# Down projections by Strassen's scheme: seven half products in place of eight

## The reference

```python
scale = cond @ norm_w.T + 1.0
h = x * (scale[:, None, :] * rsqrt(mean(x * x) + EPS))
val, gate = split(h @ up_w.T, 2)              # FF = 2048
h = val * gelu(gate)
hq = act_quant(h)                             # per token, to 127 steps
wq = weight_quant(down_w)                     # -1, 0, +1 times a scale
y = hq @ wq.T + x                             # 2048 -> 512
# second block, per batch row: an adapter of width 128
Wd_b, Wu_b = Wd + dWd(cond), Wu + dWu(cond)   # dW = (cond @ Wdd.T + bdd) * 0.1
out = y + relu(y @ Wd_b.T + bd) @ Wu_b.T + bu
```

## Time and profile before

| | us |
|---|---|
| median of 3 runs | 850.45 |
| the profiled execution, span | 847.8 |
| TensorE busy | 834.7 |
| VectorE busy | 605.6 |
| ScalarE busy | 388.4 |
| GpSimd busy | 74.3 |
| down matmuls L1182, 384 of them, busy | 84.8 |

### The profile page before, as it was taken

The page is one execution under the profiler, slowest core; times in us unless marked ns, Lnnn a source line. Parts: engine busy times, 40 slices in busy tenths (PEclk is TensorE's granted clock), DMA queues, the critical chain, the costliest instruction groups (busy, mean ns, idle before and its releaser), DMA issues.

```text
span 847.8 us, 11801 instructions
## 1 busy us (share of the span) xinstructions
PE 834.7 (98%) x3982; PEld 366.9 (43%) x3982; DVE 605.6 (71%) x904; ACT 388.4 (46%) x633; POOL 74.3 (9%) x79
## 2 busy tenths in 40 slices
PE   6999999999999999999999999999999999999998
PEld 4334444444444444444444444444444444444443
DVE  5998787989877765658776656668975664445986
ACT  5778887775454532237454542126333332224000
POOL 0363332202000000002000000000200000000100
PEclk9999999999999999999999999999999999999999
DMA  9879988665999843377889754436246444432232
GB/s 342 333 269 339 348 285 300 235 224 209 323 350 373 305 149 117 116 255 274 294 308 335 270 200 134 151 106 211 84 133 217 137 162 141 140 117 77 99 123 76
DMA packets 64426, 183.49 MB, mean 216 GB/s; under 512 B 7024, under 2 KB 8304, under 8 KB 64368
## 3 DMA queue, kind: packets, MB, share of 16 engines
q1 hardware_dynamic: 64080, 182.48, 61.7%
q10 hardware_dynamic: 288, 0.26, 0.1%
HBM read 152.31 MB, written 29.36 MB: 214 GB/s over the span
## 4 chain that ended last, share of the span: by engine, by line
PE 93%; DVE 1%; issue 0%; DVEq 0%
PE aux_ps L1182 10%; PE b_ps L1082 9%; PE b_ps L1086 9%; PE b_ps L1084 9%; PE a_ps L1082 6%; PE a_ps L1086 6%; PE a_ps L1084 6%; PE aux_ps L1137 6%; PE aux_ps L1233 3%; PE aux_ps L1224 3%; PE c_ps L1086 3%; PE c_ps L1082 3%; PE c_ps L1084 3%; PE e_ps L1082 3%; PE e_ps L1086 3%; PE e_ps L1084 3%
## 5 line engine op out<-in xcount | busy, mean ns | idle before, releaser
L1590 DVE SCALAR_TENSOR_TENSOR h_ring<-v_sb,unscale,gelu 128x512 f32<-128x512 f32 x63 | 50.9, 808 | 101.2 <-ACT gelu L885 53.4
L861 ACT ACTIVATE b_ps<-a_ps 128x512 f32<-128x512 f32 x63 | 36.7, 583 | 140.4 <-PE a_ps L1086 140.3
L1082 PE MATMUL b_ps<-t_mov,u_l 128*128 128x512 f16 x252 | 95.5, 379 | 0.6 <-DVE c_ps L1551 0.6
L1086 PE MATMUL b_ps<-t_mov,u_l 128*128 128x512 f16 x252 | 95.5, 379 | 0.0
L1084 PE MATMUL b_ps<-t_mov,u_l 128*128 128x512 f16 x252 | 95.5, 379 | 0.0
L1614 DVE TENSOR_TENSOR hmax<-gelu,hmax 128x512 f32<-128x512 f32 x120 | 82.8, 691 | 7.6 <-ACT gelu L891 2.5
L1182 PE MATMUL aux_ps<-h_ring,wq 128*128 128x512 f16 x384 | 84.8, 379 | 0.0
L753 POOL PARTITION_ALL_REDUCE yscale<-hmax x8 | 17.9, 2266 | 601.3 <-DVE hmax L1614 600.7
L895 ACT ACTIVATE gelu<-h_ring 128x512 f32<-128x512 f32 x64 | 40.3, 630 | 56.5 <-DVE h_ring L1590 56.5
L891 ACT ACTIVATE gelu<-h_ring 128x512 f32<-128x512 f32 x64 | 40.2, 629 | 52.5 <-DVE h_ring L1600 52.4
L1600 DVE SCALAR_TENSOR_TENSOR h_ring<-b_ps,unscale,gelu 128x512 f32<-128x512 f32 x64 | 47.9, 749 | 18.9 <-PE b_ps L1086 18.7
(11 more groups left out here) (225 smaller groups left out, 1620.0 us busy)
## 6 DMA issues: line engine op xcount, KB each, us to landing
w_ring<-in_Wdu SPq DMA_DIRECT2D x64, 512.0 KB, 6.1
w_ring<-in_Wdd SPq DMA_DIRECT2D x56, 512.0 KB, 6.9
u_l<-ul_dram SPq DMA_DIRECT2D x48, 512.0 KB, 4.5
u_e<-ue_dram SPq DMA_DIRECT2D x48, 384.0 KB, 3.1
h_ring<-in_up_w SPq DMA_DIRECT2D x16, 512.0 KB, 6.7
x_sb<-in_x SPq DMA_DIRECT2D x8, 1024.0 KB, 8.0
res<-in_down_w SPq DMA_DIRECT2D x16, 512.0 KB, 7.1
ul_dram<-u_l SPq DMA_DIRECT2D x15, 512.0 KB, 5.6
```

What stands on the lines that cost most here:

```text
L1082: pe.matmul(ps[:, :], weight(n, p, 0, k), hi, start=fresh and k == 0, stop=False, skip_group_check=True)
L1086: mm = pe.matmul(ps[:, :], weight(n, p, 1, k), hi, start=False, stop=k == 1, skip_group_check=True)
L1590: dve.scalar_tensor_tensor(out=h_slot(n)[:, TB:TS], in0=val[:, :], scalar=unscale[:, s // 2, j:j + 1], in1=gelu2[:, :], op0=ALU.mult, op1= ...
```

## The change

For superblocks 0 to 2 (computed in quads j = 10 to 13 of s = 1 to 3) the product W (512 x 2048) by tokens (2048 x 1024) is cut in two along each side: output rows (c: halves of 256 rows), FF (halves of 8 chunks, HC) and tokens (the two blocks). Seven half products, each for two row groups h of 8 matmuls, replace eight. Quad 10 ("c11") computes P1 and adds P2 in the same bank, quad 11 P3 ("p3"), quad 12 ("c21") P6 on a seed of P1, then P7, then P4 in the same bank, quad 13 P5 ("p5"). Between these, ACT copies banks out (`keep_p1`, `keep_p3`, `keep_u3`) and in (`seed_down`), and DVE adds U2 to the kept P3 (`add_u2`), scales and adds x for each quarter. The token sums are made in place on DVE (`token_sums`, four instructions of 128x1024 fp16 for each of four sums, m = 1, 3, 2, 4). The four weight sums (fp8) are made once, on POOL, in superblock 1 (`down_sums`: 16 rounds of four 128x128 instructions and one DMA of 64 KB to `ws_dram`, each round waiting for the DMA before it), and loaded into tiles 2 and 3 of `w_ring` before each use (`load_sums`, 1 MB). For that, the two loads of the second group of quad 30 come later in SP's queue; `load_ad(3)` also comes later. `DOWN_QUANTISE` shifts seven of eight quantisations one quad earlier. For s > 0 both "rs" units lie in quad 11, behind P3; the second `x_scaled` comes after the running maxima of quad 12. The copy targets are `stage` (P1), `qscale` (P3) and `res[:, 2:4]` (P7). The matmuls against `ones` in `stat` use a column of their own, and `spread_rs` writes its four transposes as one group. The diff, cut to its core:

```diff
+AFTER_DOWN = 2 * groups_of_quad(30)[0]
...
-DOWN_QUANTISE = (0, 3, 4, 5, 6, 7, 8, 9)
+DOWN_QUANTISE = (0, 2, 3, 4, 5, 6, 7, 8)
...
-SPREAD = {11: 0, 12: 1}
+SPREAD = {11: (0,), 12: (1,)}, {11: (0, 1)}
+DOWN_BANKS = ("c11", "p3", "c21", "p5")
...
+PAIR_ORDER = (0, 4, 1, 5, 2, 6, 3, 7)
...
+        work += [(DOWN_BANKS[j - Y_FIRST], s - 1, h) for h in range(2)]
...
+                if n in (AFTER_DOWN + 2, AFTER_DOWN + 3):
+                    aux_ready(sp, "p5", 0, 1)
...
+            def load_c21(d):
+                for h in range(2):
+                    sp.wait_ge(s_x_c12, 2 * d + h + 1)
+                    sp.dma_start(res[:, h, :], rows_x(2 * d, 2 + h)).then_inc(s_res[h], 16)
...
+            def load_sums(d, first, last):
+                if d == 0:
+                    sp.wait_ge(s_wsum_put, 16 * 2 * last)
...
+                sp.dma_start(w_sums[:, first:last, :, :, :], ws_dram[:, first:last, :, :, :])\
+                    .then_inc(s_wsum_load, 16)
...
+                        if 2 * g != AFTER_DOWN + 2:
+                            load_w(2 * g)
+                            load_w(2 * g + 1)
...
+                    load_c11(s - 1)
+                if s > 0 and j == Y_FIRST + 1:
+                    put_c11(s - 1)
+                if s > 0 and j == Y_FIRST + 3:
+                    load_c22(s - 1)
+                    load_c21(s - 1)
+                if s > 0 and j == Y_FIRST + 4:
+                    put_c21(s - 1)
                 if NP <= n + 2 < NQ:
                     load_e(n + 2)
                 if NP <= n + 1 < NQ:
                     load_l(n + 1)
...
+                if s > 0 and j == Y_FIRST:
+                    load_sums(s - 1, 0, 6 if s == 1 else HC)
+                if s > 0 and j == Y_FIRST + 1:
+                    if s == 1:
+                        load_sums(0, 6, HC)
+                    load_c12(s - 1)
+                if s > 0 and j == Y_FIRST + 4:
+                    if AFTER_DOWN // 2 in groups_of_quad(n):
+                        load_w(AFTER_DOWN + 2)
+                        load_w(AFTER_DOWN + 3)
+                    put_second(s - 1)
...
+            def down_sums(c, h):
...
+                pool.wait_ge(s_wq, 2 * (c // 2) + 2)
+                if r:
+                    pool.wait_ge(s_wsum_put, 16 * r)
+                pool.tensor_tensor(s1, a21, a22, ALU.add, saturate=False)\
+                    .then_inc(s_wsum, 1)
...
+                pool.dma_start(ws_dram[:, c, h, :, :], sum_rows).then_inc(s_wsum_put, 16)
...
+            def keep_p3(d):
+                for h in range(2):
+                    aux_ready(act, "p3", d, h)
+                    act.activation(kept3(h), bank("p3", d, h)[:, :], ACT.Copy)\
+                        .then_inc(s_keep3, 1)
...
+            def seed_down(d):
+                for h in range(2):
+                    act.wait_ge(s_keep1, 2 * d + h + 1)
+                    act.wait_ge(*bank_free(aux_keys[aux["c21", d, h] - 2]))
+                    act.activation(bank("c21", d, h)[:, :], kept1(h), ACT.Copy)\
+                        .then_inc(s_seed_down, 1)
...
+                if s > 0 and j == Y_FIRST:
+                    keep_p1(s - 1)
+                if s > 0 and j == Y_FIRST + 1:
+                    keep_p3(s - 1)
+                if s > 0 and j == Y_FIRST + 2:
+                    seed_down(s - 1)
+                    keep_u3(s - 1)
...
-            def down(i, k):
...
-                for c in range(NP):
+            def down_product(ps, d, p, h, fresh):
...
+                for c in range(HC):
...
+            def down_c11(d):
+                for h in range(2):
+                    ps = take("c11", d, h)
...
+                    down_product(ps, d, 1, h, True).then_inc(s_p1_down, 1)
+                for h in range(2):
+                    pe.wait_ge(s_keep1, 2 * d + h + 1)
+                    down_product(bank("c11", d, h), d, 2, h, False).then_inc(s_aux, 1)
+            def down_p3(d):
+                for h in range(2):
+                    ps = take("p3", d, h)
+                    pe.wait_ge(s_wsum_load, 16 * (d + 2))
+                    down_product(ps, d, 3, h, True).then_inc(s_aux, 1)
+            def down_c21(d):
+                pe.wait_ge(s_tq[2], 4 * (d + 1))
+                for h in range(2):
+                    pe.wait_ge(s_seed_down, 2 * d + h + 1)
+                    down_product(take("c21", d, h), d, 6, h, False).then_inc(s_p6_down, 1)
+                pe.wait_ge(s_tq[3], 4 * (d + 1))
+                for h in range(2):
+                    pe.wait_ge(s_u2_added, 2 * d + h + 1)
+                    down_product(bank("c21", d, h), d, 7, h, False).then_inc(s_p7_down, 1)
+                pe.wait_ge(s_tq[4], 4 * (d + 1))
+                for h in range(2):
+                    pe.wait_ge(s_keep7, 2 * d + h + 1)
+                    down_product(bank("c21", d, h), d, 4, h, False).then_inc(s_aux, 1)
+            def down_p5(d):
+                pe.wait_ge(s_tq[1], 4 * (d + 1))
+                for h in range(2):
+                    down_product(take("p5", d, h), d, 5, h, True).then_inc(s_aux, 1)
...
+            def token_sums(d, m):
+                for p in range(HC // 2):
+                    b11, b12 = q_pair(d, p, 0), q_pair(d, p, 1)
+                    b21, b22 = q_pair(d, HC // 2 + p, 0), q_pair(d, HC // 2 + p, 1)
+                    if m == 1:
+                        dve.wait_ge(s_p1_down, 2 * d + 2)
+                        args = b11, b12, b11
...
+                    dve.tensor_tensor(*args, ALU.subtract).then_inc(s_tq[m], 1)
+            def add_u2(d):
+                for h in range(2):
+                    dve.wait_ge(s_keep3, 2 * d + h + 1)
+                    dve.wait_ge(s_p6_down, 2 * d + h + 1)
+                    dve.tensor_tensor(kept3(h), bank("c21", d, h)[:, :], kept3(h), ALU.add)\
+                        .then_inc(s_u2_added, 1)
+            def scaled_c12(d):
...
+                    link(dve.tensor_tensor(kept3(h), kept3(h), second, ALU.mult))
...
+                    dve.tensor_tensor(kept3(h), kept3(h), res[:, h, :], ALU.add)\
+                        .then_inc(s_x_c12, 1)
+            def second_rows(d):
...
+                    link(dve.tensor_tensor(p5[h], p5[h], second, ALU.mult))
...
-                    if key[0] == "y":
-                        residual(key[1], (key[2],))
-                    elif key[0] == "rs":
+                    if key[0] in ("c11", "c21"):
+                        half_row(*key)
+                    elif key[0] == "p5" and key[2] == 1:
+                        second_rows(key[1])
+                    elif key[0] == "rs" and not (s and key[1] % 2):
                         x_scaled(key[1])
...
+                if s > 0 and j == Y_FIRST + 2:
+                    token_sums(s - 1, 2)
...
+                if s > 0 and j == Y_FIRST + 1:
+                    token_sums(s - 1, 1)
+                    token_sums(s - 1, 3)
+                if 0 < s < NSB - 1 and j == Y_FIRST + 2:
+                    x_scaled(2 * s + 3)
...
+                if s > 0 and j == Y_FIRST + 2:
+                    add_u2(s - 1)
+                    token_sums(s - 1, 4)
+                    scaled_c12(s - 1)
+                    scaled_c22(s - 1)
```

More of the change, by code:

```diff
@@ L760, in _ @@
                 weight_sums(j)
-            for n in range(NP, NQ, NP):
-                all_h(n // NP - 1)
-            all_h(NSB - 1)
+            all_h(0)
+            for c in range(HC):
+                for h in range(2):
+                    down_sums(c, h)
+            for s in range(1, NSB):
+                all_h(s)
         @block.scalar
@@ L1637, in scales @@
                 step(half)
+                if s >= 2:
+                    dve.wait_ge(s_c12_put[t], 16 * (s - 1))
                 inverse(half)
```

279 lines of the change are left out of this document (212 added, 67 removed).

## The result

The changed kernel takes 871.6 us (median of four runs, 868.3 to 874.2) against 850.5 us: 1.025 times the time before, with an interval of 1.022 to 1.028. The forecast was 856.4 us, its range 850.5 to 866: slower as foreseen, but by 21 us and not by 6, and outside the range. The profiled execution is the quickest of the four, 868.3 us.

What follows compares the result with a forecast made beforehand. TensorE's order of instructions bounds the kernel. Matmuls saved, -10.4 us, and waits of 0.9, 3.9, 1.7, 1.5, 2.9, 3.5 and 1.9 gave +6.0: span 853.8, plus 2.65 around it, 856.4 us; range 850.5 to 866.

Steps and rivals of the forecast that it cites:

- What it removes: Down projection: seven half products for eight, 16 matmuls less in each of three superblocks, 10.4 us, all on TensorE's path.
- Point 1: Second "rs" of quad 11, superblocks 1 and 2: TensorE waits for keep_p3 to free the bank, 0.9 us in all.
- Points 2 and 3: TensorE waits in quad 12: for seed_down before P6, 3.9 us in all; for seed_c in superblock 2, 1.7 us.
- Point 4: Token sum 4 before P4: ready 3.4 us after P6's end, while P7 runs for 3.45 us, so no wait.
- Point 5: Quads 13 and 14 of superblock 2: VectorE's work outlasts TensorE's, waits of 0.9 and 0.6 us, sum 1.5 us.
- Point 6: Superblock 1: second load of weight sums stands behind load_l(28) in SP's queue, P3 waits 2.9 us (0.8 to 3.3).
- Point 7: Quad 30: two loads of the second "dw" group stand behind load_l(31), a wait of 3.5 us (0.6 to 6).
- Point 8: down_quantise, new in quad 18, beside POOL's first weight sums: P7(19) waits 1.9 us (1.1 to 2.5).
- Hidden, if that holds.: POOL's sixteen rounds of weight sums: 5.2 us each (3.5 to 7), may take 6.0 each, so no wait.
- rival C: POOL's rounds take over 6.0 us; at 6.5 P3 waits 8 us more: 864 us; chance 0.11.
- rival D: Waits before P3 and quad 30's second "dw" group lower TensorE's clock, 2.5 us more each: 859 to 861.5; chance 0.11.
- The 2.65 us around the span: Time outside the span in the kernel before (847.8 against 850.45 us), added to the forecast span of 853.8 us.

Runs made afterwards that it cites:

- e6: e4 with all superblock 1 sums in one load in quad 26, plus ScalarE's seed copies before gate1 and x_scaled before running_max: 844.9 us.
- e7: e4 with all superblock 1 sums in one load in quad 26, plus VectorE's four assembly steps moved to quads 43, 46 and 47: 846.7 us.
- e1: Changed kernel with GpSimd's rounds of weight sums writing by turns into two buffers: 861.2 us.
- e4: Changed kernel with the edits of e1 and e2 together: 853.8 us.
- e3: Changed kernel with each position of quad 30's first adapter group run four times over, 24 more matmuls: 868.2 us.
- e2: Changed kernel with the two w_ring loads for quad 30's second group put ahead of the next quad's loads in SyncE's queue: 863.5 us.
- e9: Kernel with the edits of both e6 and e7, plus VectorE's second down-weight quantising step moved from quad 18 to quad 17: 843.1 us.
- e12: e9 with GpSimd's first pair of rounds begun after VectorE's third quantising step, not after the second: 841.2 us.

## Why the prediction was wrong

**What it removes: right.** Quads 29, 59 and 61 have a step of -3.45 us each, the price of 16 matmuls. In each of the three superblocks two quads (27 and 29, 43 and 45, 59 and 61) have 16 matmuls less than before and the one between them has 16 more. That is 3.45 us net a superblock, and 10.4 us in all.

**Point 1: right.** Quad 43 has -2.55 us: -3.45, +0.44 for a row scale that moved here from the next quad, +0.45 of waiting.

**Points 2 and 3: right but for half a microsecond.** Quad 28 has 4.44 us: 3.45 less 0.44 for the row scale, and 1.4 of waiting (1.35 expected); quad 60 has 1.1 (1.2); quad 44 has 2.7 us for both points (3.05). The runs e6 and e7 show the two parts by their places: ScalarE's order and the assembly step. Point 4: right, P4 follows P7 without a wait.

**Point 5: right in sum.** 0.73 and 0.73 us, for 0.9 and 0.6.

**Point 6: right in mechanism, a little small.** Without the chain P3's wait is 3.4 us (e1) and 3.6 us (e4) for 2.9, just above the 3.3 that the point gave as its upper end: the load took 5.4 and 5.6 us to land, for 4.95.

**Point 7: right in mechanism, its size too small.** The first half of the group waits 4.03 us, and by e3 the two loads together cost 5.3 us at full clock, for 3.5: they took 7.0 and 7.9 us to land for 6.1, and the halves no longer run side by side. e2 shows that it was the place in the queue.

**Point 8: 1.6 us for 1.9, and half understood.** Quantising and contention were both in the sum. That contention alone costs as much in this quad (1.9 us in e9), so that both have to go, is what e9 and e12 showed; quantising without GpSimd's sums beside it was not run. One reading was loose: the GpSimd row of 1.21 us at 112.03 and the VectorE row of 1.21 us at 114.94 do not overlap. The latter ran beside another GpSimd instruction, of 0.91 us. The size came out near all the same.

**The step that failed: "Hidden, if that holds."** Point 6 took SyncE's place in the order as what sets the load's time, and the prediction covered GpSimd's rounds under it: 5.2 us a round, with 6.0 as the threshold. The arithmetic in it was right (2.4 us measured, 2.6 taken). The mis-sized term is the store: 2.0 us to landing and 0.6 to issue in the sum of 5.2, against 4.3 us measured (6.74 less 2.4; landings of 3.8 to 6.0 us from 229 to 300 us). The 2.0 us came from the earlier trace rows, a store at 738 to 743 us, where the DMA share was 0.29; from 229 to 300 us it was 0.94 in the same trace, and the loads of `w_ring` took up to 8.8 us there. The price for a store had to be taken from a row of the stretch where it would stand: once the DMA share had fallen, from 303.7 us on, a round did take the 5.2 us of the prediction, but by then eight rounds had taken 8.0. So rival C came true: 6.74 us a round in the mean, P3's wait 11.0 us and not 2.9. That is 8.1 us.

**And rival D with it.** P3's 16 matmuls took 1.3 us more than at full pace, quad 30's "dw" group and what follows it 1.1 us more: 2.4 us for 5.0 expected if it held. The Trainium skill's rule (TensorE: Matmul & The Clock Gate, Part 1), that an idle engine goes back to 1.2 GHz, agrees with both places of the trace.

With these terms, in spans: 853.8 + 8.1 (C) + 2.4 (D) + 1.8 (point 7) = 866.1 us, against 866.6 us in the trace. The rest of the prediction's sum holds to 0.5 us, though some of that is small differences cancelling: 0.3 us less in point 8, 0.5 us before quad 19. (The prediction's terms add up to +5.9, not +6.0, and those of point 5's first wait to 12.3, not 12.2; nothing hangs on either.) The 2.65 us around the span are too many for this kernel: the profiled execution lies 1.7 us above its span (868.3 against 866.6), and so do those of its variants. The remaining distance to the median of 871.6 us fits the scatter of the chain of stores, which in e2's trace ended 4.2 us later and had a longer loss of clock behind it.

**The range** failed for a reason of its own. I had given C and D 0.11 each and priced each on the forecast alone. But they aren't independent: a longer wait is just what makes D true, so C's case is C with D, 864 + 5 us or nearly that, and outside the range. A chain whose own estimate (5.2, 3.5 to 7) straddles its threshold (6.0) also had more than 0.11 coming to it.

## What to carry to other kernels

Where a chain of transfers, each waiting for the one before, is said to be hidden, price each link from the stretch in which it will run, and put the threshold beside the upper end of that price; a second buffer (here 10 us) costs less than the doubt. Price rivals together when one brings the other about. And an algorithm that saves 10 us of matmuls may be judged only when its new steps stand in the right places: the same seven products gave 871.6 us and 841.2 us, by a second buffer and the order of some ten instructions in four queues.
